# An edge network's MLP pass: 2 of 32 columns per iteration from an on-chip table, half of the one-hots on ScalarE, and loops with a hint for the branch back

## What is computed

```
h = relu(layernorm(x)); x = x + L0(h, edge_weight)     # 3 times: sum of weight * ht[src]
h = relu(layernorm(x)); x = x + L1(h, edge_attr_16)    # attention over the edges of a node
h = relu(layernorm(x)); x = x + L2(h, edge_attr_8)     # sum of MLP([h[src], h[dst], attr])
h = relu(layernorm(x)); x = x + L3(h)                  # attention
```

```
msg = relu(concat([x[src], x[dst], edge_attr]) @ W1 + b1) @ W2 + b2
out = segment_sum(msg, dst)
```

## Time and profile before

| | |
|---|---|
| median of 3 runs | 14734.09 us (14725.0 to 14737.74) |
| profiled execution | 14738.15 us |
| its span | 14736.1 us |
| mean granted TensorE clock | 0.671 |
| POOL busy | 10586.9 us (72%) |
| DVE busy | 10167.6 us (69%) |
| PE busy | 9514.2 us (65%) |
| ACT busy | 4152.8 us (28%) |

### The profile page before, as it was taken

The page is one execution under the profiler, slowest core; times in us unless marked ns, Lnnn a source line. Parts: engine busy times, 40 slices in busy tenths (PEclk is TensorE's granted clock), DMA queues, the critical chain, the costliest instruction groups (busy, mean ns, idle before and its releaser), DMA issues.

```text
span 14736.1 us, 379076 instructions
## 1 busy us (share of the span) xinstructions
PE 9514.2 (65%) x89162; PEld 8562.9 (58%) x89163; DVE 10167.6 (69%) x46548; ACT 4152.8 (28%) x13780; POOL 10586.9 (72%) x10932
## 2 busy tenths in 40 slices
PE   0000007777778888788887888887555555888887
PEld 0000006777767777677776777776444444777777
DVE  7870007777776666766667787878766766888887
ACT  1000000000000000000002777776222222777777
POOL 3777777777767777677776777775777776777776
PEclk9985558888888888888886555555555555555555
DMA  2101112222111111111111111111111111111111
GB/s 100 26 25 26 26 28 46 41 42 41 37 27 27 27 27 27 27 27 27 27 27 27 27 26 26 26 26 20 31 28 27 28 28 28 28 27 27 27 27 27
DMA packets 500039, 447.85 MB, mean 30 GB/s; under 512 B 291533, under 2 KB 316749, under 8 KB 498254
## 3 DMA queue, kind: packets, MB, share of 16 engines
q0 software_dynamic: 349696, 337.89, 13.8%
q1 hardware_dynamic: 149454, 102.38, 2.5%
HBM read 368.39 MB, written 65.20 MB: 29 GB/s over the span
## 4 chain that ended last, share of the span: by engine, by line
PE 37%; issue 20%; DVE 18%; POOL 12%; DVEq 8%; DMA 3%; ACT 1%; POOLq 0%; ACTq 0%; SPq 0%
PE bank L1463 16%; PE bank L1438 12%; POOL packed L423 9%; DVEq L705 3%; DMA G<-table,idx 3%; POOL G L442 3%; PE bank L1520 3%; PE bank L1532 3%; DVE OH L722 2%; PE bank L1509 1%; DVE OHB L733 1%; PE bank L1451 1%; PE bank L1536 1%; DVEq L707 1%; DVE OHT L761 1%
## 5 line engine op out<-in xcount | busy, mean ns | idle before, releaser
L442 POOL DMA_INDIRECT G<-table,idx x9360 | 9063.1, 968 | 3426.3 <-issue 2429.8
L1463 PE MATMUL bank<-UZ,OHT 128*128 128x192 bf16 x15600 | 2095.3, 261 | 540.6 <-DVE OHT L761 540.6
L1438 PE MATMUL bank<-G,OH 128*128 128x64 f32 x9984 | 1674.1, 299 | 586.8 <-DVE OH L722 466.0
L423 POOL DMA_INDIRECT packed<-Y,slab_pos x1568 | 1523.6, 972 | 671.4 <-issue 495.3
L1356 ACT ACTIVATE OHB<-bank,const 128x512 bf16<-128x512 f32 x159 | 109.2, 687 | 6711.7 <-PE bank L1451 6711.7
L1463 PE MATMUL bank<-UZ,V 128*128 128x192 bf16 x14976 | 1999.0, 260 | 0.0
L1438 PEld LDWEIGHTS bank<-G,OH 128*128 128x128 f32 x9984 | 1486.9, 216 | 753.8 <-DVE OH L722 686.9
L1463 PEld LDWEIGHTS bank<-UZ,OHT 128*128 128x128 bf16 x15600 | 1511.6, 111 | 580.3 <-DVE OHT L761 558.0
L1438 PE MATMUL bank<-ZR,OH 128*128 128x65 f32 x6656 | 1765.4, 419 | 0.0
L1438 PEld LDWEIGHTS bank<-ZR,OH 128*128 128x128 f32 x6656 | 1623.6, 334 | 0.2
L722 DVE TENSOR_SCALAR OH<-const,DL,W 128x128 f32<-128x128 f32 x4992 | 1560.6, 368 | 0.2 <-issue 0.2
(11 more groups left out here) (281 smaller groups left out, 18624.1 us busy)
## 6 DMA issues: line engine op xcount, KB each, us to landing
G<-table,idx POOLq DMA_INDIRECT x9360, 2.5
packed<-Y SPq DMA_DIRECT2D x42, 640.0 KB, 17.6
UZ<-packed SPq DMA_DIRECT2D x104, 256.0 KB, 2.7
Y<-in_payload SPq DMA_DIRECT2D x98, 256.0 KB
packed<-Y,slab_pos POOLq DMA_INDIRECT x1568
table<-Y SPq DMA_DIRECT2D x6, 1690.0 KB, 5.5
idx<-SRC SPq DMA_DIRECT2D x624, 8.0 KB
X<-in_x SPq DMA_DIRECT2D x1, 1568.0 KB, 7.9
```

Of the source, the lines that this page charges most:

```text
L423: pool.indirect_dma_start(out=packed_rows, out_offset=bass.IndirectOffsetOnAxis(ap=slab_pos[:, h, c:c + 1], axis=0), in_=slab[:, h, c, :], ...
L442: pool.indirect_dma_start(out=G[:, 2 * q + c, :], out_offset=None, in_=table, in_offset=bass.IndirectOffsetOnAxis(ap=idx[:, h, j:j + 1], a ...
L1438: o = pe.matmul(ps_a[r % 2][:, 0:w], OH[:, q, c, :], parts[c], start=c == 0, stop=c == 1)
L1463: o = pe.matmul(ps_rows[c // 2][:, c % 2 * 3 * D:(c % 2 + 1) * 3 * D], tile_hot(tile)[:, c * P:(c + 1) * P], table_parts[:, tile, :, :].re ...
```

## The change

- MLP pass: POOL gathers 30 of 32 columns an iteration (ON_CHIP_E = 2). The last group's two columns come from the table on chip, as in the GCN passes: per iteration 49 one-hots of 256 columns and 98 matmuls of 192 columns in steps 0 to 12, up to four tiles a step. Even tiles' one-hots are made by DVE (25, one instruction each), odd tiles' by ACT (24, a Square and a Relu each, 1 - (tile - code)^2 cut at 0). A ring of seven one-hots lies in ZR and OH's tail. The table's three parts lie in Z and in W, made by DVE before the pass.
- The semaphores of the gathers have a third set for the MLP pass (LANDS).
- The loops of `steps` on DVE, ACT and PE are made with `hint_back_edge=True`.

```diff
@@ steps
-            with eng.Fori(1, ITER) as i:
+            with nc.Fori(1, ITER, engines=[eng.engine], hint_back_edge=True) as i:
                 body(None, i)
@@ fetched
-            return BODY - ON_CHIP // 2 if PLAN[n][0] == GCN else BODY
+            return BODY - {GCN: ON_CHIP, MLP: ON_CHIP_E, ATT: 0}[PLAN[n][0]] // 2
@@ vector
+                def tile_hots_e(i, u):
+                    here = [t_ for t_ in range(u * TILES_A_STEP, min((u + 1) * TILES_A_STEP, T)) if t_ in by_vector]
+                    if here and u == 0:
+                        v.wait_ge(code_ready_e, i + 1)
+                    for tile in here:
+                        need(v, tile_used_e, i * T + max(tile - RING_E + 1, 0))
+                        v.tensor_scalar(tile_hot_e(tile), code_e, float(tile), None, ALU.is_equal).then_inc(tile_ready_e, 1)
+                def take_rows_e(i):
+                    v.wait_ge(tile_used_e, i * T + T)
+                    need(v, h_done, i * (3 * BODY) + 3 * kb)
+                    got = ps_rows_e[:, 0:6 * D].rearrange("p (s k c) -> p s c k", s=2, k=3)
+                    q = BODY - 1
+                    v.tensor_reduce(G[:, 2 * q:2 * q + 2, 0:D], got, AX.X, ALU.add).then_inc(taken_e, 1)
...
                         go_on(first)
+                        if live(0):
+                            tile_hots_e(i, u)
+                        if live(0) and u == 3:
+                            choose_e(i + 1)
+                        if live(0) and u == 13:
+                            take_rows_e(i)
                         return
...
             three_parts(Z3, Z[:, :, :], Z[:, :, :])
+            for h, (t0, t1) in enumerate(((0, 34), (34, T))):
+                three_parts([parts_e[h][:, :, k, :] for k in range(3)], Y[:, t0:t1, 0:D], ACC[:, t0:t1, 0:D])
@@ scalar, mlp_pass
+                def codes(i):
+                    a.wait_ge(code_spread_e, i + 1)
+                    need(a, tile_ready_e, i * n_v)
+                    need(a, tile_made_e, i * n_a)
+                    a.activation(code_e, ps_code_e[:, 0:ON_CHIP_E * P], ACT.Identity, bias=own_row).then_inc(code_ready_e, 1)
+                def tiles(i, u):
+                    here = [t_ for t_ in range(u * TILES_A_STEP, min((u + 1) * TILES_A_STEP, T)) if t_ in by_scalar]
+                    if here and u == 0:
+                        a.wait_ge(code_ready_e, i + 1)
+                    for tile in here:
+                        need(a, tile_used_e, i * T + max(tile - RING_E + 1, 0))
+                        a.activation(tile_hot_e(tile), code_e, ACT.Square, scale=-1.0, bias=bins[:, tile:tile + 1]).then_inc(squared_e, 1)
+                    for tile in here:
+                        a.wait_ge(squared_e, i * n_a + (by_scalar.index(tile) + 1))
+                        a.activation(tile_hot_e(tile), tile_hot_e(tile), ACT.Relu, scale=-1.0, bias=ones[:, 0:1]).then_inc(tile_made_e, 1)
...
                             transposed(i * BODY + (u - 1), (u - 1) % 8)
+                        if not isinstance(i, int) or i < ITER:
+                            tiles(i, u)
+                            if u == 14:
+                                codes(i + 1)
@@ tensor, mlp_pass
                         part_sums(g - 6, (u - 6) % 8, (u - 6) % 4)
+                    if live(0):
+                        rows_from_table_e(i, u)
+                    if live(0) and u == 6:
+                        spread_e(i + 1)
...
+                def rows_from_table_e(i, u):
+                    if u == 0:
+                        need(pe, taken_e, i)
+                    for tile in range(u * TILES_A_STEP, min((u + 1) * TILES_A_STEP, T)):
+                        if tile in by_scalar:
+                            pe.wait_ge(tile_made_e, i * len(by_scalar) + (by_scalar.index(tile) + 1))
+                        else:
+                            pe.wait_ge(tile_ready_e, i * len(by_vector) + (by_vector.index(tile) + 1))
+                        for c in range(ON_CHIP_E):
+                            o = pe.matmul(ps_rows_e[:, c * 3 * D:(c + 1) * 3 * D], tile_hot_e(tile)[:, c * P:(c + 1) * P],
+                                          table_part_e(tile), start=tile == 0 and c == 0, stop=tile == T - 1 and c == 1)
+                        o.then_inc(tile_used_e, 1)
```

More of the change, by code:

```diff
@@ L52 @@
 ON_CHIP = 4
+ON_CHIP_E = 2
+RING_E = 7
 SLOTS = 8
@@ L265, in build @@
         idx_ready = [sem("idx_ready0"), sem("idx_ready1")]
-        gathered = [[sem(f"gathered{h}_{q}") for q in range(BODY)] for h in range(2)]
+        gathered = [[sem(f"gathered{h}_{q}") for q in range(BODY)] for h in (0, 1, 2)]
+        taken_e, squared_e, tile_made_e, tile_ready_e = sem("taken_e"), sem("squared_e"), sem("tile_made_e"), sem("tile_ready_e")
+        chosen_ready_e, code_spread_e, code_ready_e = sem("chosen_ready_e"), sem("code_spread_e"), sem("code_ready_e")
+        tile_used_e = sem("tile_used_e")
         go = sem("go")
@@ L770, in take_rows, with i_of, choose_e @@
                         v.tensor_reduce(G[:, 2 * q:2 * q + 2, 0:D], got, AX.X, ALU.add).then_inc(taken[k], 1)
+                passed = [0]
+                def i_of(g, q):
+                    return passed[0]
+                def choose_e(i):
+                    need(v, code_spread_e, i)
+                    at = i * (2 * BODY) + (2 * BODY - ON_CHIP_E)
+                    move(chosen_e, SRC[:, ds(at, ON_CHIP_E)]).then_inc(chosen_ready_e, 1)
+                def tile_hots_e(i, u):
[11 more added lines that the diff above has]
+                    v.tensor_reduce(G[:, 2 * q:2 * q + 2, 0:D], got, AX.X, ALU.add).then_inc(taken_e, 1)
                 def need_rows(g, q):
-                    v.wait_ge(gathered[n // LAYERS][q], (g - q) * (32 // BODY) + (landed(n) + 32))
+                    if kind == MLP and q == BODY - 1:
+                        v.wait_ge(taken_e, i_of(g, q))
+                        return
+                    v.wait_ge(gathered[LANDS[n]][q], (g - q) * (32 // BODY) + (landed(n) + 32))
                 def group_max(g, r, t):
@@ L980, in run_pass @@
                     choose(0)
+                if kind == MLP:
+                    choose_e(0)
                 clear_sums()
@@ L1347, in body @@
                             transposed(i * BODY + (u - 1), (u - 1) % 8)
+                        if not isinstance(i, int) or i < ITER:
+                            tiles(i, u)
+                            if u == 14:
+                                codes(i + 1)
+                codes(0)
                 steps(a, body, 1)
@@ L1597, in step, with spread_e @@
                         part_sums(g - 6, (u - 6) % 8, (u - 6) % 4)
+                    if live(0):
+                        rows_from_table_e(i, u)
+                    if live(0) and u == 6:
+                        spread_e(i + 1)
+                def spread_e(i):
+                    pe.wait_ge(chosen_ready_e, i + 1)
+                    need(pe, code_ready_e, i)
+                    for c in range(ON_CHIP_E):
+                        o = pe.matmul(ps_code_e[:, c * P:(c + 1) * P], chosen_e[:, c:c + 1].to_broadcast([P, P]), ident,
+                                      start=True, stop=True)
+                    o.then_inc(code_spread_e, 1)
+                def rows_from_table_e(i, u):
[6 more added lines that the diff above has]
+                            pe.wait_ge(tile_ready_e, i * len(by_vector) + (by_vector.index(tile) + 1))
+                        for c in range(ON_CHIP_E):
+                            o = pe.matmul(ps_rows_e[:, c * 3 * D:(c + 1) * 3 * D], tile_hot_e(tile)[:, c * P:(c + 1) * P],
+                                          table_part_e(tile), start=tile == 0 and c == 0, stop=tile == T - 1 and c == 1)
+                        o.then_inc(tile_used_e, 1)
+                spread_e(0)
                 steps(pe, with_tiles(step), 6)
```

31 lines of the change are left out of this document (25 added, 6 removed).

## The result

The changed kernel takes **15373.66 us** (median of 4 runs, 15369.43 to 15376.19), the kernel before 14731.44 us beside it: a ratio of 1.0436, 95% interval 1.0422 to 1.0451. It is slower by 642 us, where 1081 were forecast, and lies 26 us under the range. The profiled execution took 15373.68 us.

The account below looks back on a forecast made before the run. POOL's gathers were taken to bound the GCN and MLP passes, the attention passes nearly so. 14738 + 1238 (MLP iterations) + 10 (table split) - 170 (hint, attention passes) = 15816, said as 15815 us; range 15400 to 16150.

Parts of the forecast that it names:

- What bounds before, and which link breaks: POOL's gathers bind GCN and MLP passes, attention nearly; in MLP steps 0 to 11 PE would wait for ACT.
- The loop of 4.3 us a step: MLP pass: chain PE, ACT's evictions and four ACTIVATEs, PE's six matmuls; 4.3 us a step, formerly 1.65, for eleven steps.
- The rest of an iteration: MLP iteration outside the eleven 4.3 us steps: 17.1 us of the 64.4, with step 12 at 1.9, 13 and 14 at 3.3.
- the higher clock: MLP pass: denser matmuls bring PE to 2.4 GHz, 3.5 us a step, about 15360 us; 16% together with the 3.8 us step.
- the spread: MLP step 6: spreading the next columns by two fp32 matmuls of 275 ns, 0.5 us an iteration.
- the ring: MLP pass: the ring of seven one-hots doesn't bind, as DVE waits only for tiles PE used in step u-2.
- The boundary's 5.3: DVE's gap between MLP iterations: 7.8 us before, 5.3 with the hint, which was given 2.5 us.
- the hint gives nothing: Rival: no gain from the hint, +170 in attention passes and 130 in the MLP pass, 16116 us; chance 12%.
- The hint in the attention passes: Hint saves 2.5 us at DVE's branch, so nearly all of POOL's lost 124 + 60 us comes back: -170 us.
- POOL stays the bound: Rival: the new work hides, MLP iterations fall to 38.1 us, 14448 us in all; chance 4%.
- the change is neutral in sum: Rival: gains and losses cancel if an MLP step came to about 2.2 us; chance 1%.
- A step of 3.8: Rival for the MLP loop: ACTIVATEs at the eviction's price, 15530 us; most of 16% shared with the clock case.

Follow-up runs that it names:

- ACT's tiles first: Changed kernel with ACT making its odd tiles ahead of the evictions of the step before: 14484.92 us, ratio 0.9826; again on another chip 14475.61 us.
- all tiles by DVE: Changed kernel with all one-hots made by DVE and none by ACT: 14706.64 us, ratio 0.9973 to the kernel before.
- the hint alone: Kernel before with only hint_back_edge=True added on the loops of steps(): 14565.55 us, ratio 0.988.
- Square alone: Changed kernel with ACT's Relu of each odd tile left out, so results are not the wanted ones: 14666.57 us, ratio 0.9955.

## Why the prediction was wrong in size, by its own steps

- **What bounds before, and which link breaks:** right. PE waits in steps 0 to 11 for ACT's Relu, and POOL for DVE. The GCN passes were put at no change and took 12 us more. Cutting the one link gives 38.5 us an iteration; that is shown, since the kernel with ACT's tiles first does all of the same work.
- **The loop of 4.3 us a step was the failed step.** It measured 3.72 at the lower clock. PE's start to ACT's eviction was put at 1.31 from the earlier trace rows and was 0.99. That way held a wait for DVE: in the kernel before PE's attributes wait in most steps for DVE's copy E8S, 0.2 us each, as the waits of the kernel before say:

```profile
PEld bank L1562 <- DVE E8S L497: 147.1, 637, 0.3
```

  From the step's first matmul to PE's attributes it was 0.90 us (L1568 to L1562), and 0.64 in the changed kernel (L1659 to L1653), where DVE stands waiting for PE and has its copy ready. The iteration's start is only a small part of it: steps in the middle of an iteration had 1.23. With the evictions' 0.28 and 0.16 the first Square begins at 1.43, not 1.79. From start to start the ACTIVATEs took 0.40 and not 0.46; one lasts 0.51, as taken from L1315. The first Relu ends at 1.43 + 0.79 + 0.50 = 2.72, not 3.22, and PE goes on at 2.78, not 3.3. The last six matmuls took 0.94 (0.96). That is 0.58 us a step too much, x 11 x 52 = 332 of the 441 us by which the forecast was off. ScalarE: Activation LUTs, What ACT_TABLE_LOAD costs, in the Trainium skill, gives 0.40 from start to start, as an estimate from its figures (0.49 for one, 0.09 of it overlapped). On that term the trace agrees with the page (0.40), where the prediction took the row's duration less a guessed overlap.
- **The rest of an iteration** was 2.2 us too long as well. Step starts of PE in one iteration, changed kernel (steps 0, 1, 12, 15 and the next 0):

```profile
11212.33 0.23 PE L1659 MATMUL bank<-WE,E8T 128*128 128x128 bf16 x1 [2.10 <-issue]
...
11219.70 0.31 PE L1659 MATMUL bank<-WE,E8T 128*128 128x128 bf16 x1
...
11260.36 0.31 PE L1659 MATMUL bank<-WE,E8T 128*128 128x128 bf16 x1
...
11263.91 0.29 PE L1659 MATMUL bank<-WE,E8T 128*128 128x128 bf16 x1
...
11267.19 0.23 PE L1659 MATMUL bank<-WE,E8T 128*128 128x128 bf16 x1 [2.21 <-issue]
```

  Steps 12 to 14 together took 3.55 us and not 5.8: they were priced at DVE's pace of 1.65, but DVE is ahead by then and PE runs at its own, about 1.1. Step 15, the boundary and step 0 took 10.65 (10.8 forecast). Steps 1 to 11 took 40.66, 7.1 less than forecast: 332 / 52 = 6.4 of that is the loop above, and most of the rest the higher clock in steps 7 to 10, which the prediction had as a rival for the whole pass; against these the spread cost 0.9 and not 0.5. This iteration is 54.9 us, one of the four shortest; in most of the others steps 7 to 10 took 3.72 too, and the mean iteration is 55.8. So an iteration was forecast 8.6 us too long: 6.4 by the loop, 2.4 by the rest, 0.4 by the clock, and the spread and steps 1 to 3 take 0.6 back.
- **Setup, ring, boundary:** the table's split took 11 us (10 forecast), and no wait for the ring shows. The boundary's 5.3 was right, but its reason wasn't: the 2.5 us (130 of the sum) that the prediction gave to the hint in the MLP pass came from the loop's new place, since the kernel without the hint has them too. For the same reason the rival "the hint gives nothing" was mispriced: 16116 less the forecast is 301, and the measured worth is 190. Runtime: NRT & Kernel Launch, Instruction fetch mechanics, in the Trainium skill, makes such a branch wait where its target isn't in the window of two pages that the engine holds; that a shift of 25 instructions makes and unmakes the gap agrees with it, while no run here shows the window itself. With the hint the longest gap was 0.9 us in most kernels, but 1.9 in the last attention pass with all tiles by DVE.
- **The hint in the attention passes:** predicted 170 us, measured 180 in the two attention passes (103 and 77), from which the GCN passes take 12; 180 in all with the hint alone, 190 and 199 by its removal. The gap fell to 0.75 us, as forecast (under 1). That POOL's waits would all be 0.30 was nearly so: 25 us are left in pass 3.
- **The rivals' sums** had two slips, neither of which moved the forecast. POOL stays the bound below 1.91 us a step, which was called less than the 1.86 of PE's way to ACT and the evictions, and is more. And the change is neutral in sum at about 2.4 us a step, since 15816 less 14738 is 1078 and a step counts 572 times; 2.2 leaves out the hint and the split.
- **The range** had its lower end at 15400 since 3.5 us a step was given a small share. A step of 3.8, its ACTIVATEs at the eviction's spacing, was the cheaper bound from rows, and the true lead of 0.99 was below any that had been set: the lead was taken from one row as it stood, with a wait in it that the new loop doesn't have, and got no lower bound.

## What to carry to other kernels

When work is handed to an idle engine, ask what stands ahead of it in that engine's order. ACT had over 70% to spare, and still cost 4.4%, because its new work stood behind a wait for the engine that needs it; with the same work ahead of that wait the kernel is 1.7% faster than before, of which the hint alone is 1.2. Price such a loop link by link, take out of each link the waits that the new loop won't have (here DVE's copy, 0.26 us of the lead), and bound the links that look certain too. And when the bound engine has no longer waits and still is slower, look at how long its own instructions take: with all tiles by DVE POOL's gathers went from 0.99 to 1.11 us. A hint for the branch back costs one word and is worth up to 3 us an iteration on an engine whose loop binds; without it the price hangs on where the loop happens to stand, so that an unrelated edit can move the time by 0.6% (20197.56 against 20073.86 us, single runs on a slower chip).

## What the runs showed of the hardware that had not been expected

- With plain loops the gap of a loop's branch back on DVE is either about 3 us or about 0.4, by the loop's place alone: 3.02 with 8 instructions ahead, 0.38 with 25, for the same body. With the hint it was 0.32 to 0.43 in the MLP pass of every kernel and about 0.77 in attention pass 3. In the last attention pass it still differed: 0.46 with the hint alone, 0.75 in the changed kernel, 1.67 with all tiles by DVE.
- TensorE's granted clock in the MLP pass differed from kernel to kernel: 0.50 before, 0.56 changed, 0.77 with all tiles by DVE, 0.82 with ACT's tiles first, 0.87 with Square alone. The length of an iteration alone doesn't set it (all tiles by DVE and Square alone both have 42.1 us). Inside the changed kernel it rose behind the two fp32 products of the spread in 18 of 51 iterations. Where PE's waits for ACT were cut or shortened the clock was higher too, so the cut paid twice here.
- POOL's gathers aren't of one length: 0.94 us mostly, but up to 1.68 beside runs of three or four one-hots on DVE, a mean of 1.11 with all tiles by DVE.
- Two ACTIVATEs of 128x256 between SBUF tiles that last 0.51 us each begin 0.40 us apart.
- The slower chips gave about the same clocks, and DVE's own instructions the same durations, but stalls ended by "remote", which no trace of the usual chips has. They stand in every kernel traced there, on DVE, ACT and POOL. In the kernel before with 25 instructions ahead of the loop, DVE stalls about 6.4 us a few steps apart in the MLP pass; its timeline:

```profile
14019.06 0.22 DVE L870 TENSOR_TENSOR ACC<-ACC,bank 128x65 f32 x1 [6.39 <-remote]
```

  Its MLP iteration takes 59.1 us with POOL waiting for DVE. What these stalls are stays open.
